# Softmax without dividing the probabilities: row-sum reciprocals applied to the attention output, and earlier high-half copies in batch 0

## What is computed

```
q, k = _rms_norm(q, g_q), _rms_norm(k, g_k)          # 16 heads of 32 features
logits = jnp.einsum('bhqd,bhkd->bhqk', q, k) * d ** (-0.5)
attn = jax.nn.softmax(logits, axis=-1)
o = jnp.einsum('bhqk,bhkd->bhqd', attn, v)
return o + o @ W_out                                  # then x + ffn(...)
```

## Time and profile before

| | us |
|---|---|
| median of 3 runs (range) | 3059.54 (3057.57 to 3059.79) |
| profiled execution, its own time | 3062.81 |
| its span in the trace | 3061.1 |
| TensorE products busy | 2788.1 (91%) |
| VectorE busy | 1827.7 (60%) |
| ScalarE busy | 1121.8 (37%) |
| GpSimd busy | 1354.7 (44%) |
| mean granted TensorE clock | 0.921 |

### The profile page before, as it was taken

One profiled execution on the slowest core, in us unless ns is written; L12 is line 12 of the kernel. 1 busy time (PEld: TensorE's weight loads), 2 busy tenths in 40 slices (PEclk: granted clock), 3 DMA queues, 4 the chain that ended last, 5 costly groups with the idle time before them and its releaser, 6 DMA issues.

```text
span 3061.1 us, 132271 instructions
## 1 busy us (share of the span) xinstructions
PE 2788.1 (91%) x48208; PEld 2427.2 (79%) x48208; DVE 1827.7 (60%) x6585; ACT 1121.8 (37%) x4950; POOL 1354.7 (44%) x3466
## 2 busy tenths in 40 slices
PE   6778989889888556999999999999999999999998
PEld 4346667667767455999999899899899899899987
DVE  2657656755764444666666666666666666566654
ACT  1224433644552223333333333333333333333321
POOL 1220000111110666666666566566566566666600
PEclk7569999999999555999999999999999999999999
DMA  4523222533441000344444444444444344344466
GB/s 142 171 80 107 82 86 58 176 125 114 141 147 32 25 0 0 112 126 131 131 130 129 123 129 131 125 129 128 124 130 128 121 131 130 109 145 127 132 217 198
DMA packets 137163, 359.87 MB, mean 118 GB/s; under 512 B 15888, under 2 KB 24720, under 8 KB 136592
## 3 DMA queue, kind: packets, MB, share of 16 engines
q1 hardware_dynamic: 136336, 354.17, 37.8%
q10 hardware_dynamic: 672, 3.67, 0.3%
HBM read 323.31 MB, written 34.47 MB: 117 GB/s over the span
## 4 chain that ended last, share of the span: by engine, by line
PE 61%; DVE 2%; issue 2%; ACT 1%; DVEq 0%; DMA 0%; POOL 0%; POOLq 0%; SPq 0%
PE pscan L1234 13%; PE pscan L1230 13%; PE pg L1161 11%; PE pd L1187 11%; PE pu L1161 11%; ACT th L1088 1%; DVE state L1350 1%; DVE carry L1350 0%; PE prouter L1245 0%; DMA wd<-w_split 0%; PE prouter L1253 0%; PE pd L1260 0%; DVE pscan L1336 0%; DVEq L1349 0%; DVE th L1333 0%
## 5 line engine op out<-in xcount | busy, mean ns | idle before, releaser
L1230 PEld LDWEIGHTS pscan<-th,carry 128*128 128x128 f16 x16384 | 555.7, 97 | 135.6 <-ACT th L1088 114.9
L1230 PE MATMUL pscan<-th,carry 128*128 128x8 f16 x16384 | 564.4, 167 | 100.6 <-ACT th L1088 100.4
L1234 PE MATMUL pscan<-th,carry 128*128 128x16 f16 x16384 | 561.9, 170 | 3.0 <-DVE th L1333 2.3
L1234 PEld LDWEIGHTS pscan<-th,carry 128*128 128x128 f16 x16384 | 486.8, 97 | 4.5 <-DVE th L1333 4.5
L1088 ACT ACTIVATE th<-state 128x32 f16<-128x32 f32 x768 | 176.1, 229 | 733.0 <-DVE state L1350 733.0
L1161 PE MATMUL pg<-qh,wgu 128*128 128x256 f16 x3168 | 430.1, 275 | 14.5 <-issue 14.5
L1187 PE MATMUL pd<-hg,wd 128*128 128x256 f16 x3168 | 428.9, 274 | 2.8 <-DMA wd<-w_split 2.8
L1161 PE MATMUL pu<-qh,wgu 128*128 128x256 f16 x3168 | 429.2, 275 | 1.9 <-issue 1.8
L1350 DVE TENSOR_REDUCE state<-pscan 128x32 f32<-128x96 f32 x768 | 197.1, 257 | 268.0 <-PE pscan L1234 262.8
L1161 PEld LDWEIGHTS pg<-qh,wgu 128*128 128x128 f16 x3168 | 295.5, 98 | 53.3 <-issue 15.9
L1161 PEld LDWEIGHTS pu<-qh,wgu 128*128 128x128 f16 x3168 | 295.0, 98 | 37.1 <-issue 2.6
(11 more groups left out here) (203 smaller groups left out, 4573.3 us busy)
## 6 DMA issues: line engine op xcount, KB each, us to landing
wgu<-w_split SPq DMA_DIRECT2D x264, 512.0 KB, 3.6
wd<-w_split SPq DMA_DIRECT2D x264, 384.0 KB, 3.1
parts_mem<-in_w_tiles SPq DMA_DIRECT2D x120, 256.0 KB, 3.0
w_split<-parts_mem SPq DMA_DIRECT2D x99, 256.0 KB, 2.2
late<-in_w_tiles SPq DMA_DIRECT2D x78, 256.0 KB, 3.2
w_split<-late SPq DMA_DIRECT2D x33, 128.0 KB, 3.0
out<-oo SPq DMA_DIRECT2D x8, 512.0 KB, 4.0
xs<-in_x SPq DMA_DIRECT2D x1, 3584.0 KB, 13.2
```

The source lines that it names most:

```text
L1230: mm(pscan[:, 0, m * B:(m + 1) * B], clo[:, k, m * P:(m + 1) * P], th[:, k, 0, :], start=(m == 0 and k == 0), stop=False, skip_group_check ...
L1234: ins = mm(pscan[:, 0:2, m * B:(m + 1) * B], chi[:, k, m * P:(m + 1) * P], th[:, k], start=False, stop=(k == NC - 1), skip_group_check=True)
```

## The change

Five things change together.

1. `normed` is gone: the undivided exponentials are turned, and `transposed(h)` waits for ScalarE's exponentials alone. VectorE inverts the sums of four heads at once (`inverse(c)`).
2. In `weighted(c)` TensorE first makes 8 more products: the reciprocals of a head and half of the queries, broadcast to 32 columns as the stationary operand, by the unit matrix. They write the reciprocals, spread over 32 partitions for each head and 256 queries, into the second half of Ob.
3. ScalarE copies that half to `oT` (`widened`), and VectorE multiplies the first half by it (`gathered` is now VectorE's). The output product and the sum wait for VectorE's signal.
4. The input norm of the next batch moves ahead: squares at the end of chunk 0, its sum after head 5 (into Ob[1]), `norm` at the end of chunk 1, `normed_input` at the end of chunk 2. `weighted(1)` waits until `norm` has read Ob[1]. The condition products at the start use Ob[0] instead of Ob[1].
5. In batch 0 ScalarE copies the high half of piece h+4 in chunk c = h/4 itself: the first of four after the exponentials of the third head, the other three after those of the fourth.

```
 ScalarE
-                    if not ffn and 3 <= h and h + 1 < PIECES:
-                        weights_high(h + 1)
+                def pieces(h, count):
+                    for piece in range(h + NC, min(h + NC + count, PIECES)):
+                        if not ffn:
+                            weights_high(piece)
-                def gathered(c):
+                def widened(c):
                     act.wait_ge(S["p_pv"], b * NC + c + 1)
-                    act.activation(oT[:, c, :], Ob[c % 2][:, 0:T], ACT.Copy).then_inc(S["a_oT"], 1)
+                    act.activation(oT[:, c, :], Ob[c % 2][:, T:2 * T], ACT.Copy).then_inc(S["a_wide"], 1)
                     exps(HPC * c + 2)
+                    pieces(HPC * c, 1)
                     relus(ffn_quad[c][2:3])
                     exps(HPC * c + 3)
+                    pieces(HPC * c + 1, HPC - 1)
                     relus(ffn_quad[c][3:])
+                    if c == 0 and b + 1 < B:
...
                         squares(b + 1)
+                    if c == 1 and b + 1 < B:
+                        norm(b + 1)
+                widened(NC - 1)
 TensorE
                 def transposed(h):
-                    pe.wait_ge(S["d_pn"], b * HEADS + h + 1)
+                    pe.wait_ge(S["a_exp"], b * HEADS + h + 1)
                 def weighted(c):
+                    if c == 1 and more:
+                        pe.wait_ge(S["a_rstd"], b + 2)
                     if c >= 2:
-                        pe.wait_ge(S["a_oT"], b * NC + c - 1)
+                        pe.wait_ge(S["d_oT"], b * NC + c - 1)
+                    pe.wait_ge(S["d_rinv"], b * NC + c + 1)
+                    for qc in range(2):
+                        for j in range(HPC):
+                            mm(Ob[c % 2][DH * j:DH * (j + 1), T + qc * P:T + (qc + 1) * P], rinv[:, HPC * c + j, qc:qc + 1].to_broadcast([P, DH]), ident[:],
+                               start=True, stop=True)
 VectorE
-                def normed(h):
-                    dve.wait_ge(S["a_exp"], b * HEADS + h + 1)
-                    dve.reciprocal(rinv[:, h, :], psum_e[:, h, :]).then_inc(S["d_rinv"], 1)
-                    dve.wait_ge(S["d_rinv"], b * HEADS + h + 1)
-                    for qc in range(2):
-                        ins = dve.tensor_scalar(pr[:, h % HPC, qc, :], pr[:, h % HPC, qc, :], rinv[:, h, qc:qc + 1], None, ALU.mult)
-                    ins.then_inc(S["d_pn"], 1)
+                def inverse(c):
+                    dve.wait_ge(S["a_exp"], b * HEADS + HPC * (c + 1))
+                    dve.reciprocal(rinv[:, HPC * c:HPC * (c + 1), :], psum_e[:, HPC * c:HPC * (c + 1), :]).then_inc(S["d_rinv"], 1)
+                def gathered(c):
+                    dve.wait_ge(S["a_wide"], b * NC + c + 1)
+                    dve.tensor_tensor(oT[:, c, :], Ob[c % 2][:, 0:T], oT[:, c, :], ALU.mult).then_inc(S["d_oT"], 1)
```

More of the change, by code:

```diff
@@ L149, in layer0 @@
                  "p_nrm p_qk p_hr p_v p_s p_t p_pv p_wo p_up p_dn x_biased "
-                 "a_sqx a_rstd a_sq a_hr a_v a_exp a_oT a_relu a_up a_x1 a_whi "
-                 "d_xn d_qk d_max d_rinv d_pn d_pt d_sum d_span g_span d_scale d_x1 d_up d_x2 "
+                 "a_sqx a_rstd a_sq a_hr a_v a_exp a_wide a_relu a_up a_x1 a_whi "
+                 "d_xn d_qk d_max d_rinv d_pt d_oT d_sum d_span g_span d_scale d_x1 d_up d_x2 "
                  "chain achain seq plseq "
@@ L383, in norm @@
                 act.wait_ge(S["p_nrm"], b + 1)
-                act.activation(rs[:, 0, :], Ob[0][:, T:2 * T], ACT.Ln, scale=1.0 / N, bias=eps).then_inc(S["achain"], 1)
+                act.activation(rs[:, 0, :], Ob[1][:, T:2 * T], ACT.Ln, scale=1.0 / N, bias=eps).then_inc(S["achain"], 1)
                 act.wait_ge(S["achain"], b * 5 + 1)
@@ L442, in batch @@
                     if c:
-                        gathered(c - 1)
-                    if c == NC - 1 and b + 1 < B:
-                        norm(b + 1)
+                        widened(c - 1)
                     relus(ffn_quad[c][0:2])
                     exps(HPC * c + 2)
+                    pieces(HPC * c, 1)
                     relus(ffn_quad[c][2:3])
                     exps(HPC * c + 3)
+                    pieces(HPC * c + 1, HPC - 1)
                     relus(ffn_quad[c][3:])
-                    if c == NC - 2 and b + 1 < B:
+                    if c == 0 and b + 1 < B:
                         if b == 0:
@@ L470, in norm_sum @@
                 for k in range(NC):
-                    ins = mm(Ob[0][:, T:2 * T], ones[:], sq[:, k, :], start=(k == 0), stop=(k == NC - 1))
+                    ins = mm(Ob[1][:, T:2 * T], ones[:], sq[:, k, :], start=(k == 0), stop=(k == NC - 1))
                 ins.then_inc(S["p_nrm"], 1)
@@ L478, in _ @@
                 for k in range(NC):
-                    ins = mm(Ob[1][:, m * B:(m + 1) * B], w_emb[:, k, m * P:(m + 1) * P], condT[:, k, :], start=(k == 0), stop=(k == NC - 1))
+                    ins = mm(Ob[0][:, m * B:(m + 1) * B], w_emb[:, k, m * P:(m + 1) * P], condT[:, k, :], start=(k == 0), stop=(k == NC - 1))
             ins.then_inc(S["mm_ss"], 1)
@@ L595, in batch @@
                         weighted(c - 1)
-                    if c == NC - 1 and more:
-                        norm_sum(b + 1)
                     for part in ffn_quad[c][0:2]:
@@ L606, in batch @@
                             ffn_part(b - 1, ffn_quad[c][2 + j])
+                        if (c, j) == (1, 1) and more:
+                            norm_sum(b + 1)
                 weighted(NC - 1)
@@ L613, in batch @@
                     pe.wait_ge(S["wo_in"], 16)
-                pe.wait_ge(S["a_oT"], b * NC + NC)
+                pe.wait_ge(S["d_oT"], b * NC + NC)
                 for m in range(NC):
@@ L766, in batch @@
                     row_max(h + 1)
-                    normed(h)
                     row_max(h + 2)
-                    normed(h + 1)
+                    if c:
+                        gathered(c - 1)
                     turned(h)
@@ L772, in batch @@
                     row_max(h + 3)
-                    normed(h + 2)
                     turned(h + 1)
                     lows(b, ffn_quad[c][2:3])
-                    normed(h + 3)
                     turned(h + 2)
-                    if c == NC - 1 and b + 1 < B:
-                        normed_input(b + 1)
+                    inverse(c)
                     turned(h + 3)
                     lows(b, ffn_quad[c][3:])
+                    if c == 2 and b + 1 < B:
+                        normed_input(b + 1)
                     if ffn and c == NC - 1:
                         second(b - 1, 0)
+                gathered(NC - 1)
                 for i in range(2):
```

7 lines of the change are left out of this document (2 added, 5 removed).

## The result

The changed kernel takes 3013.3 us (median of four runs, 3004.7 to 3016.5) against 3059.7 before: a ratio of 0.9845, 95% interval 0.9824 to 0.9866. That is 46 us less, where 30 were forecast; the forecast range ended at 3016. Two repeats gave 0.9846 (0.9828 to 0.9864) and 0.9842 (0.9828 to 0.9855).

The account below looks back on a forecast made before the run. TensorE was taken as the bound in batches 1 to 7, a chain of hand-offs in batch 0. 28.8 - 15.4 - 2.0 = 11.4 us plus 18.5 made 29.9 less: 3030 us, forecast 3023 to 3038, range with rivals 3016 to 3045.

Parts of the forecast that it names:

- Idle time that goes in batches 1 to 7: TensorE's waits before transposes and value products in batches 1 to 7: 28.8 us go, 2.0 us of new waits come.
- The waits of 4.6 to 5.6 us before the first transposed heads of batches 4 to 7: Not caused by the division: 0.8 us of each goes, 17.0 of 20.2 us stay.
- The waits of about 2 us in batches 1 to 3: TensorE's wait for the first transposed head, 1.96 us in batch 1, goes whole with the division.
- the 18.0: TensorE's idle us before the product with the values, ended by the last copy, all said to go with the moved norm.
- wait before `weighted(1)`: TensorE waits there for `norm`: 0 to 0.3 us, part of 2.0 us for all new waits.
- The new products: 8 products with the unit matrix in each chunk of batches 1 to 7: 0.55 us a chunk, 15.4 us added.
- The rival in which they do not overlap: The new products take 2.6 us a chunk instead of 0.55, so the kernel is slower, 3103 us; chance 0.05.
- The term that failed: TensorE in batches 1 to 7: the bound, at clock 0.96 in batch 1; no gain counted from its clock.
- Batch 0: A chain of hand-offs whose four chunks fall from 111.1 to 92.6 us, 18.5 us less.
- the fetch hides: In batch 0 a buffer's way takes 10.6 us, less than the 15.8 us until it is wanted again.
- the rival of the clock: TensorE's clock rises in batch 0, half of 12 low-rank products 1.9 us shorter, 11 us more go: 3019; chance 0.13.
- GpSimd beside L674: In batch 0 L674 keeps 1.22 us when GpSimd's subtractions overlap it; GpSimd takes 2.94 instead of 2.13.

Follow-up runs that it names:

- experiment 7: The changed kernel with 2 instead of 3 weight parts of layer 1 in each of the first four slots of batches 4 to 7: ratio 0.9788.
- experiment 12: The kernel before with 2 instead of 3 weight parts of layer 1 in the first four slots of batches 4 to 7: ratio 0.9954.
- experiment 3: The changed kernel without the 8 products of reciprocals in each chunk, so the attention is not normalised: 3010.8 us, ratio 0.9838.
- experiment 2: The kernel before with TensorE's idle time in batches 1 to 7 filled with products into an unused half bank: ratio 0.9986.
- experiment 9: The changed kernel with 7 filler products in the wait before the first transposed head of batches 4 to 7: ratio 0.9858.
- experiment 4: The changed kernel with batch 0's high-half copies where they were before: 3029.7 us, batch 0 114.3 us.
- experiment 5: The kernel before with the early high-half copies of batch 0 alone: ratio 0.9935, batch 0 107.2 us.
- experiment 6: The changed kernel with the next batch's input norm back in chunk 3: 3028.9 us, batches 1 to 7 721.0 us.

## Why the prediction was wrong

The direction and the two places were right; the size was not (30 us forecast, 46 to 48 measured). The step that failed is in batches 1 to 7, 11.4 us forecast and 26.1 measured: the prediction took away idle time and added the new products, and left TensorE's busy time on all other products as it was, at no price. Step by step:

- **Idle time that goes in batches 1 to 7** (28.8 us, less 2.0 for new waits): measured 25.6 net. The sum comes this close partly by luck, as two errors cancel. The waits of 4.6 to 5.6 us before the first transposed heads of batches 4 to 7 were to keep 17.0 us and kept 14.3 (they are 3.3 to 3.9 us now). The waits of about 2 us in batches 1 to 3 were to go whole, and 0.9 to 1.3 us of each stayed, 3.3 in sum. The ground of the first reading was right, as experiments 7 and 12 show: another 13.5 us lie there, with or without the change. The 2.8 us of batch 0 inside the 18.0 were counted in the wrong place. No wait before `weighted(1)` was seen.
- **The new products** (15.4 us): 0.46 us a chunk start to start, so 12.9 us of TensorE's time; taking them out wins 7 to 9 us. This term was over-sized by 2.5 us at least. The rival in which they do not overlap is out. The Trainium skill, "TensorEngine Tiling (Array Packing)", section "Instruction Overhead", gives each matmul about 60 cycles of overhead; on top of each of the 16 passes that would have been 0.4 us a chunk more, and the 0.46 us measured leave no room for it.
- **The term that failed: TensorE's busy time on the old products in batches 1 to 7.** The prediction read a clock of 0.96 in batch 1 and gave it no price; it weighed the clock only in batch 0. Apart from the new products TensorE's busy time in batches 1 to 7 fell by 13.4 us: 659.1 before, 658.5 after, of which 12.9 are new. Per batch this is 1.0 to 2.5 us. So the sum is 25.6 + 13.4 - 12.9 = 26.1 us.
- **The clock is about half of that term.** It went from 0.95 to 0.98 up to 0.98 to 1.00. Length times missing clock (unrounded), summed over the seven batches, fell from 18.8 to 6.8 us, so the clock can be 12 us of it at most. At equal clock 0.8 to 1.0 us a batch are left, 5 to 7 us in seven batches, by the rows at clock 1.00 above. That leaves 6 to 8 us for the clock, an estimate from these rows. What the 5 to 7 us are is open. A part may be this: a feed-forward pass lasts 277 ns, but twelve take 1.47 us, so the next starts some 0.11 us after it, and before a wait the last pass counts some 0.17 us in full. Three waits fewer in a batch would be 0.5 us, an estimate from these two numbers.
- **Where in a batch it was won.** Cut at the first and at the last transposed head, the seven batches became shorter by 8.7 us before the first, 2.0 us between them, and 15.4 us behind the last. Between them a loss was forecast: 21 of the 28 sets of new products stand there, 11.6 us at the forecast's price, with few waits to go. It did not come, and this is most of the error. The forecast had TensorE as the bound there. But in batches 1 to 3 of the kernel before this part took 45.8 us in every trace, at the low clock or at full clock: VectorE's chain, with the division in it, set the pace, and where TensorE ran slow its waits did not show as idle time. So the waits read in the rows were fewer than those that the division caused. With the division gone the part took 45.2 us with the new products, and 43.9 without them (experiment 3). Behind the last transposed head 3.3 us are the slow stretches of batches 1 and 4 that are gone, in time and not only in busy time.
- **What is not shown.** The edit takes the division out and brings the clock up together. The clock alone was tried (experiments 2 and 9); the division alone, with the clock kept low, was not.
- **Batch 0** (18.5 us): the stretch is 20.2 us shorter in the first trace, 23.5 and 23.7 in the repeats. The chunks were forecast at 25.0, 26.8, 28.8 and 12.0 us. The first of these was said to run from the first row maximum, but its 27.9 us of before run from the first scores at 88.10; cut there, the four took 26.7, 25.8, 27.2 and 11.4 us. Chunk 0 thus won 1.2 us instead of 2.9, and the others more than forecast. The early copies were the main term (experiments 4 and 5), the fetch hides but for 1.8 us, and L718, now L727, is stretched as forecast (3.53 us against 1.54). The rest is the rival of the clock, in part: the clock of the stretch was 0.61 to 0.65 against 0.56, and a few low-rank products took 2.0 to 2.4 us instead of 3.8. They run right behind a burst of TensorE (scores, new and value products, or the sum of squares); that this burst is the reason is argued and was not tried.
- **GpSimd beside L674**: I went by one row, in which VectorE started first. The Trainium skill, "GPSIMD Engine Reference", section "Specifications", says that the two share the SBUF interfaces, with contention for VectorE instructions with two SBUF inputs. The trace agrees where GpSimd had started first: 2.66 us instead of 1.22. It happened twice in chunk 0 (2.66 and 1.83 us), 2.1 us together, against 1.7 us that chunk 0 was longer than forecast.
- **Layer 1** gave 6 us in the first trace, by its spread. The forecast had rightly nothing for it.

## What to carry to other kernels

When the bound engine's row shows a clock below full, put a price on it: compare the same instruction's duration at both levels and count it, and ask of each idle gap that goes whether a slow stretch goes with it. But that price is due only if nothing else waits behind the slow stretch; filling the gap with idle products tests this, if the stages are compared and not the totals. The other side of it: where a slow stretch stands before waits on another engine, the idle time that you read there is less than that engine costs. And look at what stays of a wait after an edit: here the larger part of the waits before the first transposed heads of batches 4 to 7 came from too many weight parts ahead of the scores, and one number there was worth another 14 us.

## What was not expected of the hardware

In batch 3 of the kernel before a wait of 2.02 us before the transposes was followed by a stretch at 1.2 GHz (2.69 us instead of 1.47 for a part). In experiment 6 one of 1.5 us before value products, and in experiment 3 even one of 3.72 us before the transposes of batch 4, left the clock at 1.00. So the length of a single gap does not tell. The same slow stretch cost 1.6 us at the end of batch 1 and nothing in the chunks of batches 2 and 3. A stage that no edit touched (layer 1) spread over 2060.9 to 2067.1 us between traces, as much as the smallest effect that totals were meant to show. When a restore of VectorE and a subtraction of GpSimd meet, the one that starts second pays: 2.66 us instead of 1.22 on VectorE, 3.14 instead of 2.13 on GpSimd.
